# Cross-attention with single score banks: one exponential per key tile, four first-pass banks, alternating passes, maxima negated in their reduction

## The reference

```
q = layernorm(x) @ W_Q + b_Q ; k = ctx @ W_K + b_K ; v = ctx @ W_V + b_V
per head: s = (q k^T) / sqrt(32)            # 512 x 8192 scores
          p = exp(s - max over keys) ; o = (p @ v) / sum(p)
x = x + concat(o) @ W_O + b_O
```

## Time and profile before

| | |
|---|---|
| runs | 3680.82, 3687.98, 3688.92 us; median 3687.98 |
| profiled execution | span 3690.2 us (the page gives no other time for it) |
| PE busy | 3575.8 us (97%), 17916 matmuls |
| DVE busy | 2570.7 us (70%) |
| ACT busy | 1981.7 us (54%) |
| POOL busy | 1781.2 us (48%) |
| first attention, all heads | about 699 to 1592 us |
| second attention, all heads | about 2017 to 2909 us |

### The profile page before, as it was taken

How to read it: one execution, slowest core, us unless ns; L and a number is a source line. 1 busy time by engine, 2 the same in 40 slices (tenths; PEclk the granted TensorE clock), 3 DMA queues, 4 the chain that set the end, 5 groups by cost and what they waited for, 6 DMA issues and landing times. The chain is left out here.

```text
span 3690.2 us, 46629 instructions
## 1 busy us (share of the span) xinstructions
PE 3575.8 (97%) x17916; PEld 2313.7 (63%) x17916; DVE 2570.7 (70%) x3497; ACT 1981.7 (54%) x2320; POOL 1781.2 (48%) x744
## 2 busy tenths in 40 slices
PE   8999999999999999988999999999999897999999
PEld 6788788654554555446876545555554476788887
DVE  3222344587787787557996877877876465899998
ACT  2122322466666666634973666666666421777776
POOL 2122222489889989700001889989988320100001
PEclk9999999999999999998998999999999998999999
DMA  7777776532332332046978433333331100999998
GB/s 274 252 246 228 244 236 202 178 92 69 91 92 71 88 92 73 18 173 224 362 296 237 108 91 72 89 92 77 83 92 31 52 1 20 366 376 368 379 377 302
DMA packets 249723, 628.46 MB, mean 170 GB/s; under 512 B 43632, under 2 KB 137872, under 8 KB 194976
## 3 DMA queue, kind: packets, MB, share of 16 engines
q1 hardware_dynamic: 210720, 552.08, 46.2%
q10 hardware_dynamic: 36864, 67.13, 4.9%
q0 software_dynamic: 1920, 6.29, 0.5%
HBM read 488.46 MB, written 136.87 MB: 169 GB/s over the span
## 5 line engine op out<-in xcount | busy, mean ns | idle before, releaser
L790 DVE TENSOR_REDUCE maxima<-psum 128x1 f32<-128x512 f32 x2048 | 1286.1, 683 | 344.2 <-PE psum L785 341.6
L961 POOL TENSOR_TENSOR exp_sums<-pt 128x1024 f32<-128x1024 f32 x342 | 816.8, 2389 | 296.0 <-PE psum L834 147.1
L785 PE MATMUL psum<-ks,first_q 96*128 96x512 f32 x2048 | 805.4, 434 | 4.8 <-DMA ks<-k_parts 0.6
L949 ACT ACTIVATE pt<-psum 128x1024 f32<-128x1024 f32 x704 | 717.6, 1026 | 142.7 <-PE psum L814 116.2
L964 POOL TENSOR_TENSOR exp_sums<-exp_sums,pt 128x1024 f32<-128x1024 f32 x310 | 737.4, 2379 | 44.4
L830 PE MATMUL psum<-pt,vs 128*32 128x512 f32 x4096 | 675.6, 600 | 7.1 <-issue 2.3
L785 PEld LDWEIGHTS psum<-ks,first_q 96*128 96x128 f32 x2048 | 386.9, 189 | 455.2 <-DVE maxima L790 318.1
L834 PE MATMUL psum<-exp_sums,constants 128*32 128x512 f32 x1408 | 671.4, 600 | 0.0
L814 PE MATMUL psum<-qs,ks 97*128 97x512 f32 x2048 | 656.2, 404 | 3.1 <-PEq L87 3.1
L1660 DVE TENSOR_TENSOR moe_cut<-moe_raw,moe_cut 128x2048 fp32r<-128x2048 f32 x244 | 556.9, 2290 | 55.9 <-ACT moe_cut L1656 48.6
L1656 ACT CAST moe_cut<-moe_raw 128x2048 fp32r<-128x2048 f32 x244 | 468.9, 1923 | 55.5 <-PE psum L97 47.0
(11 more groups left out here) (337 smaller groups left out, 4835.3 us busy)
## 6 DMA issues: line engine op xcount, KB each, us to landing
moe_raw<-in_moe_w SPq DMA_DIRECT2D x244, 1024.0 KB, 8.3
ks<-k_parts SPq DMA_DIRECT2D x384, 256.0 KB, 4.6
k_parts<-kparts ACTq DMA_DIRECT2D x256, 256.0 KB, 4.2
cx<-in_ctx SPq DMA_DIRECT2D x32, 1024.0 KB, 6.2
vs<-v_heads SPq DMA_DIRECT2D x32, 1024.0 KB, 5.3
v_heads<-vrow SPq DMA_DIRECT2D x25, 1024.0 KB, 5.1
late_context<-cparts SPq DMA_DIRECT2D x28, 512.0 KB, 11.7
late_parts<-late_context SPq DMA_DIRECT2D x28, 512.0 KB, 4.6
```

The lines of the kernel that those rows point to most:

```text
L785: pe.matmul(self.c.bank[self.FIRST_BANK + k % 3], self.first_q[s][:, t * P:(t + 1) * P], self.ks[s][part][0:3 * DH, at:at + CHUNK], start= ...
L790: dve.tensor_reduce(self.maxima[:, h % 2, i % TT, i // TT:i // TT + 1], self.c.bank[self.FIRST_BANK + k % 3], X, ALU.max).then_inc(*self.f ...
L949: act.activation(self.pt[:, to:to + 2, :], self.c.psum[:, at:at + 2, :], ACT.Exp).then_inc(*self.exp.up())
L961: engine.tensor_tensor(to, self.pt[:, slot:slot + R, :], self.pt[:, slot + R:slot + 2 * R, :], ALU.add).then_inc(*signal.up())
```

## The change

The second pass makes one tile per bank in three single banks (4, 5, 6), and ACT takes one exponential of 512 columns for each tile, with one signal per tile. The first pass has four banks (0 to 3). In a block PE issues one unit of the first pass, one tile of the second, one unit, one tile, and so on. The maxima are reduced and negated in one DVE instruction; `col_max` and its signal are gone. The half signals are gone, and all waits that counted pairs count tiles. The projection stage moves its banks to 4 to 7 so that 0 to 3 are free for the first pass; the last transposes move from bank 4 to bank 5.

```diff
-    K_BANK, V_BANK = 3, 5
-    SPARE_BANKS = (0, 1, 2, 7)
+    K_BANK, V_BANK = 4, 6
+    SPARE_BANKS = (0, 1, 2, 3)
...
-    FIRST_BANK, SECOND_BANK, OUT_BANK = 0, 3, 7
+    FIRST_BANK, SECOND_BANK, OUT_BANK = 0, 4, 7
+    FIRST_ROOM, SECOND_ROOM = 4, 3
...
-        if k > 2:
-            pe.wait_ge(*self.first_read.at(k - 2))
+        if k >= self.FIRST_ROOM:
+            pe.wait_ge(*self.first_read.at(k - self.FIRST_ROOM + 1))
...
         if i == self.UNITS - 1:
             dve.wait_ge(*self.first_read.at(k + 1))
-            dve.tensor_reduce(self.col_max[:], self.maxima[:, h % 2], X, ALU.max).then_inc(*self.columns.up())
             if h > 1:
                 dve.wait_ge(*self.row_in[h % 2].at(TT * (h // 2)))
-            dve.wait_ge(*self.columns.at(h + 1))
-            dve.tensor_scalar(self.neg_max[:, h % 2, :], self.col_max[:], -1.0, None, ALU.mult).then_inc(*self.negated.up())
+            dve.tensor_reduce(self.neg_max[:, h % 2, :], self.maxima[:, h % 2], X, ALU.max, negate=True).then_inc(*self.negated.up())
...
-        def second_pair(h, b, i):
-            t = self.BLOCKS[b][i]
-            pair = (h * KT + t) // 2
-            after_half = i >= 4 and self.in_halves(b, i - 4)
-            for j in range(2):
-                if after_half and j == 0:
-                    pe.wait_ge(*self.half.at(self.halves(h, b)))
-                elif pair > 1 and j == (1 if after_half else 0):
-                    pe.wait_ge(*self.exp.at(pair - 1))
-                part, at = divmod((t + j) * P, self.PART)
-                last = pe.matmul(bank[self.SECOND_BANK + 2 * (pair % 2) + j], ks[h % 2][part][:, at:at + P], qs[h % 2][:], start=True, stop=True)
-                if j == 0 and self.in_halves(b, i):
-                    last.then_inc(*self.second_half.up())
-            last.then_inc(*self.second.up())
+        def second_on_pe(h, t):
+            n = h * KT + t
+            if n >= self.SECOND_ROOM:
+                pe.wait_ge(*self.exp.at(n - self.SECOND_ROOM + 1))
+            part, at = divmod(t * P, self.PART)
+            pe.matmul(bank[self.SECOND_BANK + n % self.SECOND_ROOM], ks[h % 2][part][:, at:at + P], qs[h % 2][:], start=True, stop=True).then_inc(*self.second.up())
...
-                for i in range(0, len(tiles), 2):
+                for i, t in enumerate(tiles):
                     if todo:
                         self.first_on_pe(pe, todo.pop(0))
-                    second_pair(h, b, i)
-                    if i == 2 and h + 1 == HEADS:
+                    second_on_pe(h, t)
+                    if i == 3 and h + 1 == HEADS:
                         output_early(b)
-                    if todo:
-                        self.first_on_pe(pe, todo.pop(0))
-                    if i == 2 and b == self.LAG and h:
+                    if i == 3 and b == self.LAG and h:
                         finish_head(h - 1)
...
-                    if self.in_halves(b, i):
-                        ...
-                    else:
-                        act.wait_ge(*self.second.at(pair + 1))
-                        act.activation(self.pt[:, to:to + 2, :], self.c.psum[:, at:at + 2, :], ACT.Exp).then_inc(*self.exp.up())
+                for i, t in enumerate(tiles):
+                    n = h * KT + t
+                    act.wait_ge(*self.second.at(n + 1))
+                    act.activation(self.pt[:, self.slot(h, b) + i, :], self.c.bank[self.SECOND_BANK + n % self.SECOND_ROOM], ACT.Exp).then_inc(*self.exp.up())
```

More of the change, by code:

```diff
@@ L545, in on_vector @@
         return h + 1 == HEADS and b % 2 == 1
[L547 to L555, removed]
     def sums_to(self, h, b):
@@ L575, in hold @@
         self.maxima = c.sb(st, f"maxima{l}", [P, 2, TT, self.CHUNKS])
-        self.col_max = c.sb(st, f"col_max{l}", [P, TT])
         self.neg_max = c.sb(st, f"neg_max{l}", [P, 2, TT], F32R)
@@ L585, in hold @@
         self.q_made, self.q_f, self.q_high, self.q_low = c.signals(st, "q_made q_f q_high q_low")
-        self.first, self.first_read, self.columns, self.negated, self.ones_row = c.signals(st, "first_scores first_read maxima_columns maxima_negated ones_row")
+        self.first, self.first_read, self.negated, self.ones_row = c.signals(st, "first_scores first_read maxima_negated ones_row")
     def hold_keys(self):
@@ L644, in run @@
             self.wo_in, = c.landings(st, "wo_in")
-            self.second, self.second_half, self.exp, self.half = c.signals(st, "second_scores second_half exp_done exp_half")
+            self.second, self.exp = c.signals(st, "second_scores exp_done")
             self.sum_pool, self.sum_dve, self.weighed, self.taken = c.signals(st, "sum_by_pool sum_by_dve block_weighed partial_taken")
@@ L760, in loads @@
                         self.send_row(sp, h + 1)
-                    sp.wait_ge(*self.second.at((h * KT + (part + 1) * KT // self.PARTS) // 2))
+                    sp.wait_ge(*self.second.at(h * KT + (part + 1) * KT // self.PARTS))
                     self.load_k(sp, h + 2, part)
@@ L784, in first_on_pe @@
             pe.wait_ge(*self.first_q_in[s].at(3 * (h // 2 + 1)))
-        pe.matmul(self.c.bank[self.FIRST_BANK + k % 3], self.first_q[s][:, t * P:(t + 1) * P], self.ks[s][part][0:3 * DH, at:at + CHUNK], start=True, stop=True).then_inc(*self.first.up())
+        pe.matmul(self.c.bank[self.FIRST_BANK + k % self.FIRST_ROOM], self.first_q[s][:, t * P:(t + 1) * P], self.ks[s][part][0:3 * DH, at:at + CHUNK], start=True, stop=True).then_inc(*self.first.up())
     def first_on_dve(self, dve, k):
@@ L789, in first_on_dve @@
         dve.wait_ge(*self.first.at(k + 1))
-        dve.tensor_reduce(self.maxima[:, h % 2, i % TT, i // TT:i // TT + 1], self.c.bank[self.FIRST_BANK + k % 3], X, ALU.max).then_inc(*self.first_read.up())
+        dve.tensor_reduce(self.maxima[:, h % 2, i % TT, i // TT:i // TT + 1], self.c.bank[self.FIRST_BANK + k % self.FIRST_ROOM], X, ALU.max).then_inc(*self.first_read.up())
         if i == self.UNITS - 1:
             dve.wait_ge(*self.first_read.at(k + 1))
-            dve.tensor_reduce(self.col_max[:], self.maxima[:, h % 2], X, ALU.max).then_inc(*self.columns.up())
             if h > 1:
                 dve.wait_ge(*self.row_in[h % 2].at(TT * (h // 2)))
-            dve.wait_ge(*self.columns.at(h + 1))
-            dve.tensor_scalar(self.neg_max[:, h % 2, :], self.col_max[:], -1.0, None, ALU.mult).then_inc(*self.negated.up())
+            dve.tensor_reduce(self.neg_max[:, h % 2, :], self.maxima[:, h % 2], X, ALU.max, negate=True).then_inc(*self.negated.up())
     def on_pe(self, pe):
@@ L824, in weigh @@
                 pe.wait_ge(*self.finished.at(h))
-            pe.wait_ge(*self.exp.at((h * KT + tiles[-1] + 1) // 2))
+            pe.wait_ge(*self.exp.at(h * KT + tiles[-1] + 1))
             if self.adds(b):
@@ L938, in on_act @@
                     self.ones_on_act(act, 1, self.ONES.index(b))
-                for i in range(0, len(tiles), 2):
-                    pair = (h * KT + tiles[i]) // 2
-                    at, to = self.SECOND_BANK + 2 * (pair % 2), self.slot(h, b) + i
-                    if self.in_halves(b, i):
-                        act.wait_ge(*self.second_half.at(self.halves(h, b)))
-                        act.activation(self.pt[:, to, :], self.c.bank[at], ACT.Exp).then_inc(*self.half.up())
-                        act.wait_ge(*self.second.at(pair + 1))
-                        act.activation(self.pt[:, to + 1, :], self.c.bank[at + 1], ACT.Exp).then_inc(*self.exp.up())
-                    else:
-                        act.wait_ge(*self.second.at(pair + 1))
-                        act.activation(self.pt[:, to:to + 2, :], self.c.psum[:, at:at + 2, :], ACT.Exp).then_inc(*self.exp.up())
+                for i, t in enumerate(tiles):
+                    n = h * KT + t
+                    act.wait_ge(*self.second.at(n + 1))
+                    act.activation(self.pt[:, self.slot(h, b) + i, :], self.c.bank[self.SECOND_BANK + n % self.SECOND_ROOM], ACT.Exp).then_inc(*self.exp.up())
         take_partial(HEADS - 1)
@@ L955, in add_up @@
         tiles, g, slot, R = self.BLOCKS[b], h * len(self.BLOCKS) + b, self.slot(h, b), self.ROUNDS
-        engine.wait_ge(*self.exp.at((h * KT + tiles[min((n + 2) * R, len(tiles)) - 1] + 1) // 2))
+        engine.wait_ge(*self.exp.at(h * KT + tiles[min((n + 2) * R, len(tiles)) - 1] + 1))
         to = self.sums[:, g % 2]
```

## The result

The median fell from 3686.81 us (3680.82 to 3688.92) to 3642.25 us (3640.35 to 3645.09): ratio 0.9879, 95% interval 0.9865 to 0.9893. The forecast was 3655, in 3643 to 3682. The direction, the place and the mechanism came out as forecast. The size did not: the gain is 44.6 us where I had 32, and the time lies 0.75 us outside the range, on its fast side. The step that failed is the sum of the gains.

What follows compares the result with a forecast made beforehand. PE was taken to set the pace, with stalls on DVE's reading of the maxima and on L797's wait for POOL. Savings less the last head's 4.6 us gave 16.2 an attention, 32.4 in all: 3655 us, range 3643 to 3682.

Steps and rivals of the forecast that it cites:

- the sum of the gains: Both attentions: 1.43 us for each of heads 1 to 13, plus other heads, less last head; 16.2 each, 32.4 together.
- F4's wait on the third bank: Regular block: first-pass unit F4 starts 0.12 us late, its bank still read by DVE; four banks remove this.
- the product's wait for POOL: End of each head's first pass: L797 takes 1.69 us, waiting for POOL's addition; PE's block is 0.67 longer than regular.
- Rival A: Regular blocks: POOL takes over and holds their old length, only the L797 stall goes; 9 us gained, 3679; chance 0.13.
- Rival B: Regular blocks: part of the gain, last exponential late or starts 0.24 apart, not 0.235; 15 us less, 3670; chance 0.15.
- Rival C: Each block's last second-pass tile waits for an exponential, three banks too few; at 0.68 spacing 38 us slower, 3726; chance 0.05.
- Rival D: End of first pass: the negated reduction waits for POOL as L797 did; 3658, inside the forecast; chance 0.63 together with it.
- The last head: No first-pass units fill the time, so three banks lose 0.51 us in nine of eleven blocks: 4.6 us an attention.
- The 0.09: Regular block, eight a head: 4.97 us becomes 4.89 without the bank stall, 0.09 saved with the rounding of starts.
- block behind a head's first pass: PE's block after each head's last first-pass units: 5.64 us becomes a regular 4.89, 0.75 saved.
- short and fold block: Two blocks a head, the short one and the one with fold matmuls: no stall to save, each pays 0.02 us.
- The rule on ScalarE's per-instruction cost: Second-pass exponentials: fixed latency per instruction gives 0.57 us for 512 columns without overlap; even so, no stall.

Runs made afterwards that it cites:

- e7: Changed kernel with first-pass matmuls and their reductions over 256 of the 512 keys, leaving out half the first pass's work: 3593.3 us, ratio 0.9750.
- e1: Changed kernel with the two-step negation back (reduction to col_max, then a product with -1): 3660.9 us, ratio 0.9937.
- e5: Changed kernel with a ring of four second-pass banks (3 to 6) in the last head: 3631.0 us, ratio 0.9855.
- e8: Kernel before, with only DVE's four output-bias additions moved from heads 1 to 4 to the last head: 3680.9 us, ratio 0.9986.
- e3: Changed kernel with a ring of three first-pass banks in place of four: 3687.4 us, ratio 1.0003.
- e4: Changed kernel with the old order inside a block (first, second, second, first, and so on): 3662.3 us, ratio 0.9939.
- e6: Changed kernel with a ring of two second-pass banks in place of three: 3816.2 us, ratio 1.0355.

## What the prediction had right, and the step that failed

*Which stalls, and that they go.* Right. F4's wait on the third bank and the product's wait for POOL are both gone, nothing took their place inside the heads (from 760 to 1480 us no second-pass matmul waits for ACT), and PE's starts show it. Rival A (POOL takes over) was wrong: in after no `weigh` waits for POOL in that stretch. Only e7 brings that limit out, when up to 0.64 us a block is taken from PE. Rival B was wrong: F and S alternate at 0.234, not 0.24. Rival C was wrong: exponentials start 0.49 apart. Rival D was wrong in its premise (the reduction takes 0.22 us), and its price would have been wrong too: 14 to 19 us as e1 shows, not 3.

*The last head.* Right in mechanism and size. From the block with the last first-pass units to the end of the first attention it was 76.1 us (from 1515.26) and is 80.7 (from 1489.83): 4.6, as worked out. Nine blocks of the last head pay 0.49 each and the third pays nothing, as I had it; the first even gains 0.4, and the end of the head before, which I had not looked at, loses 0.6. That these two cancel is luck. e5 takes the loss back.

*The sum of the gains.* This is the step that failed: "Heads 1 to 13: 8 x 0.09 + 0.75 - 2 x 0.02 = 1.43", with its neighbours. The 0.09 is the mis-sized term; it measured 0.11. I had 16.2 an attention; measured are 21.5 and, without the clock's 1.6, 21.3. By terms of one attention, from the blocks:

| term | forecast | measured |
|---|---|---|
| regular blocks, 104 | 0.09 each, 9.4 | 4.970 to 4.857: 0.113, 11.7 |
| block behind a head's first pass, 13 | 0.75 each, 9.8 | 5.64 to 4.86: 0.78, 10.1 |
| short and fold block, 26 | -0.02 each, -0.5 | 3.93 to 3.92 and 5.76 to 5.76: 0 |
| block behind the fold, heads 1 to 4 | as regular | 5.58 to 5.13: 0.33 more each, 1.3 |
| head 0 | 1.6 | 36.8 to 35.0: 1.8 |
| head 14, seven regular blocks | 0.6 | 0.12 each, 0.85 |
| last head | -4.6 | -4.6 |
| sum | 16.2 | 21.2 |

(The first three blocks, 16.05 to 15.84 us, give the other 0.2; part of them runs at a granted clock of 0.50 in both kernels.) Two things were at fault. I built the new block from rounded parts (0.34 + 10 x 0.235 + 0.34 + 1.86) instead of taking the old one and removing the 0.12 that I had just read. The block came out 0.03 us too long; with the 0.02 that I took off in the short and fold blocks the first three rows of the table are 3.2 us an attention too small, 6 in both. And I read one head in the middle and multiplied; heads 1 to 4 have a longer block, which the DVE addition in the same function makes, and e8 shows it: 3 us in both. Together they explain 9 of the 12 us that were missing; heads 0 and 14 add 1, and the clock dip 1.6. The range's low end allowed 9 us for a last head without loss, which did not happen, and 0.01 a block; an allowance for the reading itself was missing. Without that 9 us, which stood there for another reason, the time would lie further outside.

*The rule on ScalarE's per-instruction cost* (the Trainium skill, "VectorE: DVE Perf Modes", section "The TRN2 errata"), which by itself speaks against small tiles: it changed nothing here. The busy sum for ACT in an attention even fell by 7 us, since overlapping instructions count once.

## What to carry to other kernels

When two engines hand over banks, write down the loop (matmul, hand-over, read, hand-over) and its spacing against the issue spacing: in e3, e4 and e6 it gave the regular block to 0.02 us. Here a fourth first-pass bank is worth 45 us and a third second-pass bank 174, and the order of issue decides how many suffice. Forecast a new block as the old one less the stalls read in it, and list every block of the stage before multiplying one.

## What the runs showed of the hardware that was not expected

Some DVE instructions wait until POOL's running addition ends. The product of four numbers ended with POOL's addition in before (1244.96 against 1244.93) and in e1 (1232.66 against 1232.63), at 1.69 and 1.92 us; with POOL idle it takes 0.17. The bias addition of 0.68 us took 2.83 when POOL left no gap. The addition of the value bias in each head does it in before and after alike: 0.29 us with POOL idle, 1.66 to 1.79 in all 28 heads where POOL adds, so one such wait a head is left in the changed kernel (DVE's timeline of after; POOL's addition ran from 1248.99 to 1251.37):

```profile
1249.73 1.79 DVE L950 TENSOR_TENSOR head_rows<-head_rows,bv 128x128 f32<-128x128 f32 x1
...
1515.41 0.29 DVE L950 TENSOR_TENSOR head_rows<-head_rows,bv 128x128 f32<-128x128 f32 x1
```

Reductions of SBUF never did (219 to 224 ns in 32 cases). It goes the other way too: in e8 an addition of POOL that started while DVE was at a bias addition took 2.79 us instead of 2.38. The Trainium skill says so in "SBUF — State Buffer", section "Who interferes with whom": the pair of ports is held for the whole instruction, a tensor_scalar in a two-port mode and a tensor_tensor with two SBUF inputs contend with POOL, tensor_reduce does not. The traces agree on which instructions wait; the ports, and the mode in which the product ran, no trace shows. What follows is that an engine that becomes denser (POOL in e7) can lengthen DVE's small instructions fourfold.
